# Another order of TensorE's products within a pair of tiles

## What is computed

```python
W = weights[condition]
y = jnp.einsum('bct,bcd->bdt', x, W)
z = jnp.einsum('bsd,od->bso', y, W0) + b
u = jnp.einsum('bsd,edr->ebsr', y, A)
m = jnp.einsum('ebsr,ero,e->bso', u, B, p_scores)
norm_z = jnp.linalg.norm(z, axis=-1, keepdims=True)
norm_m = jnp.linalg.norm(m, axis=-1, keepdims=True)
gamma = jnp.minimum(0.5 * norm_z / (norm_m + 1e-6), 1.0)
out = x + z + gamma * m
```

## Time and profile before

| what | value |
|---|---|
| median of 3 runs | 920.68 us (920.51 to 920.72) |
| the profiled execution | 920.52 us, its span 918.5 us |
| mean granted TensorE clock | 0.999 |
| matmuls, busy | 908.7 us, 99% |
| weight loads, busy | 772.6 us, 84% |
| VectorE, ScalarE, POOL, busy | 587.4, 366.8, 320.6 us |

### The profile page before, as it was taken

One profiled execution on the slowest core, in us unless ns is written; L12 is line 12 of the kernel. 1 busy time (PEld: TensorE's weight loads), 2 busy tenths in 40 slices (PEclk: granted clock), 3 DMA queues, 4 the chain that ended last, 5 costly groups with the idle time before them and its releaser, 6 DMA issues.

```text
span 918.5 us, 14733 instructions
## 1 busy us (share of the span) xinstructions
PE 908.7 (99%) x4628; PEld 772.6 (84%) x4628; DVE 587.4 (64%) x930; ACT 366.8 (40%) x727; POOL 320.6 (35%) x317
## 2 busy tenths in 40 slices
PE   8999999999999999999999999999999999999997
PEld 6888888888888888888888888888888888888885
DVE  6995766566665557665566656666655766566665
ACT  6653443434334334434343343334333433433342
POOL 0123443224433234432344332444323443224432
PEclk9999999999999999999999999999999999999999
DMA  8212222122221222211222212222112222022211
GB/s 304 71 71 94 93 74 77 40 94 94 71 94 47 71 94 79 86 67 50 94 94 71 93 43 74 94 71 94 54 63 94 94 71 88 36 88 94 73 47 69
DMA packets 32744, 75.16 MB, mean 82 GB/s; under 512 B 12761, under 2 KB 13786, under 8 KB 32730
## 3 DMA queue, kind: packets, MB, share of 16 engines
q1 hardware_dynamic: 32138, 73.91, 22.7%
q10 hardware_dynamic: 592, 1.08, 0.3%
HBM read 41.42 MB, written 33.55 MB: 82 GB/s over the span
## 4 chain that ended last, share of the span: by engine, by line
PE 97%; DMA 1%; SPq 0%; DVE 0%; ACT 0%; POOL 0%; issue 0%; DVEq 0%; POOLq 0%
PE b_ps L903 37%; PE c_ps L903 19%; PE mix_ps L890 12%; PE a_ps L903 10%; PE m_ps L962 9%; PE u_ps L943 6%; PE u_ps L947 3%; PE m_ps L903 1%; DMA w_hi_raw<-in_L_ffn_W_dram 1%; POOL stats L372 0%; DMA cond_ids<-in_itok_B_dram 0%; SPq L270 0%; SPq L244 0%; ACT squares L583 0%; DVE z L882 0%
## 5 line engine op out<-in xcount | busy, mean ns | idle before, releaser
L431 ACT CAST y<-mix_ps 128x512 fp32r<-128x512 f32 x126 | 74.4, 591 | 297.9 <-PE mix_ps L890 297.9
L367 POOL TENSOR_TENSOR stats<-stats 128x1 f32<-128x1 f32 x32 | 17.7, 553 | 451.0 <-ACT squares L484 451.0
L903 PE MATMUL b_ps<-w_hi,y 128*128 128x512 f32 x512 | 168.5, 390 | 0.6 <-DVE w_lo L606 0.6
L672 DVE TENSOR_TENSOR s_lo<-s,s_hi 128x512 fp32r<-128x512 f32 x124 | 134.3, 1102 | 4.1
L890 PEld LDWEIGHTS mix_ps<-mixer,x_in 128*128 128x128 f32 x1008 | 122.0, 191 | 6.4 <-issue 1.7
L890 PE MATMUL mix_ps<-mixer,x_in 128*128 128x128 f32 x1008 | 122.7, 275 | 0.5 <-DMA mixer<-in_L_cond_weights_dram 0.5
L444 ACT CAST s_hi<-s 128x512 fp32r<-128x512 f32 x124 | 76.7, 618 | 114.7 <-POOL s L341 93.2
L353 POOL TENSOR_TENSOR z<-z,x_in 128x512 f32<-128x512 f32 x61 | 79.0, 1295 | 113.5 <-ACT squares L465 107.1
L903 PEld LDWEIGHTS b_ps<-w_hi,y 128*128 128x128 f32 x512 | 96.1, 188 | 21.2 <-ACT w_hi L415 1.0
L651 DVE TENSOR_TENSOR y<-mix_ps,y 128x512 fp32r<-128x512 f32 x126 | 86.5, 687 | 39.8 <-ACT s L437 39.6
L903 PE MATMUL b_ps<-w_lo,y 128*128 128x512 f32 x256 | 99.6, 389 | 0.0
(11 more groups left out here) (118 smaller groups left out, 1566.8 us busy)
## 6 DMA issues: line engine op xcount, KB each, us to landing
x_in<-in_x_dram SPq DMA_DIRECT2D x63, 512.0 KB, 3.5
out_dram<-z SPq DMA_DIRECT2D x62, 512.0 KB, 2.8
w_lo_raw<-in_L_ffn_W_dram SPq DMA_DIRECT2D x8, 256.0 KB, 6.2
mixer<-in_L_cond_weights_dram SPq DMA_DIRECT2D x126, 16.0 KB, 2.1
w_hi_raw<-in_L_ffn_W_dram SPq DMA_DIRECT2D x7, 256.0 KB, 6.2
out_dram<-z SPq DMA_DIRECT2D x3, 256.0 KB, 2.0
x_in<-in_x_dram ACTq DMA_DIRECT2D x1, 512.0 KB, 3.2
a_lo_raw<-in_L_ffn_A_dram SPq DMA_DIRECT2D x1, 512.0 KB, 8.1
```

The lines of the kernel that those rows point to most:

```text
L431: nc.scalar.copy(y_part(y_hi, r, h), source(h)).then_inc(y_hi_ready, 1)
L672: nc.vector.tensor_tensor(s_lo[:, n, :, :], s_raw(n), s_hi[:, n, :, :].bitcast(fp32), ALU.subtract).then_inc(s_lo_ready, 1)
L903: summed = nc.tensor.matmul(bank, left[:, k, :], right[:, n, k, :], start=(start and k == 0 and i == 0), stop=(stop and k == HC - 1 and i ...
```

## The change

TensorE's order in a pair becomes P1, P4, P2, up 0, down, mix 0, P6, P5, P7, mix 1, up 1, P3. The down product does its eight wide passes first and its eight narrow ones last, in the prologue too, where a wait on the low part of y falls away since that was waited for earlier. ScalarE squares m before it copies u. VectorE adds P4's bias ahead of `make_z11`, makes the sum of u behind `add_m0`, and makes u2 behind the two y splits of the next tile 0. For the pair p = 1 the sum of u and u2 are taken out of the prologue and made by `step` in the same places as for any other pair.

```diff
--- before.py
+++ after.py
@@ -563,8 +563,8 @@
                     square_z11(p, j, False)
                     if first:
                         split_s(p, S4, True)
+                    square_m0(p - 1, first)
                     copy_u(p, False)
-                    square_m0(p - 1, first)
                     split_u(p)
                     if not closing:
                         for h in range(2):
@@ -811,10 +811,8 @@
             nc.vector.tensor_tensor(s14[:, 1, :, :], s14[:, 1, :, :], s23[:, 0, :, :], ALU.subtract).then_inc(s4_made, 1)
             split_t(T3, 0)
             dve.wait_ge(bias_difference_ready, 1)
-            sum_u(1)
             add_p4_bias(1)
             split_t(T3, 1)
-            make_u2(1, 1)
             split_s(1, S4)
 
             def step(i, first, last):
@@ -832,17 +830,16 @@
                         bias_p1(p, j)
                         for n in (S3, S1, S4):
                             split_s(p, n)
+                        add_p4_bias(p)
                         make_z11(p, j)
-                        sum_u(p)
-                        add_p4_bias(p)
                     make_gamma(p - 1, 0)
                     add_m0(p - 1, 1 - j)
+                    sum_u(p)
                     split_u(p)
-                    if not first:
-                        make_u2(p, j)
                     if not closing:
                         for h in range(2):
                             split_y(p + 1, 0, h)
+                    make_u2(p, j)
                     make_u3(p, j)
                     dve.wait_ge(p4_biased, p)
                     dve.wait_ge(u3_ready, p)
@@ -934,22 +931,15 @@
                 pe.wait_ge(u_hi_ready, p + 1)
                 pe.wait_ge(u_lo_ready, p + 1)
 
-            def down(p):
-
-
-
-                def both(k):
-
-                    return nc.tensor.matmul(u_ps[:, :], a_hi[:, k, :], y[:, k, :, :], start=(k == 0), stop=(k == KC - 1))
-
-                both(0)
+            def down():
+
+
+
                 for k in range(KC):
-                    nc.tensor.matmul(u_ps[:, 0:2 * P], a_lo[:, k, :], y[:, k, 0, :], start=False, stop=False)
-                for k in range(1, HC):
-                    both(k)
-                pe.wait_ge(y_lo_ready, halves(2 * p + 1, 1))
-                for k in range(HC, KC):
-                    summed = both(k)
+                    summed = nc.tensor.matmul(u_ps[:, :], a_hi[:, k, :], y[:, k, :, :], start=(k == 0), stop=(k == KC - 1))
+                for k in range(KC):
+                    summed = nc.tensor.matmul(u_ps[:, 0:2 * P], a_lo[:, k, :], y[:, k, 0, :], start=False,
+                                              stop=(k == KC - 1), skip_group_check=True)
                 summed.then_inc(u_done, 1)
 
             def up(r, m):
@@ -1000,8 +990,7 @@
                 plain(bank, r, 1, W21)
             pe.wait_ge(a_hi_ready, 1)
             pe.wait_ge(a_lo_ready, 1)
-            pe.wait_ge(y_lo_ready, halves(1, 0))
-            down(0)
+            down()
             plain(c_ps[:, :], 0, 1, W22)
             pe.wait_ge(x_loaded[2], 16)
             pe.wait_ge(mixer_loaded[0], 32 * PER)
@@ -1030,16 +1019,7 @@
                         pe.wait_ge(u3_ready, p - 1)
                     product_y(b_ps, 0, 0, W11).then_inc(p_done[1], 1)
 
-                    pe.wait_ge(y_hi_ready, halves(2 * p + 1, 1))
-                    pe.wait_ge(y_lo_ready, halves(2 * p + 1, 0))
-                    down(p)
-
-                    pe.wait_ge(p1_biased, p)
-                    product_y(b_ps, 0, 1, W21, False).then_inc(p_done[2], 1)
-
-                    pe.wait_ge(out1_ready, p)
-                    up(0, m_ps)
-
+                    y_ready(2 * p + 1, 1)
                     if first:
                         pe.wait_ge(z21_ready, 1)
                         pe.wait_ge(t_hi_ready, t_count(T4, 1))
@@ -1048,15 +1028,23 @@
                         pe.wait_ge(p4_biased, p - 1)
                     product_y(a_ps, 1, 1, T4).then_inc(p_done[4], 1)
 
+                    pe.wait_ge(p1_biased, p)
+                    product_y(b_ps, 0, 1, W21, False).then_inc(p_done[2], 1)
+
+                    pe.wait_ge(out1_ready, p)
+                    up(0, m_ps)
+
+                    down()
+
+                    if not closing:
+                        mix_next_0(i, j, p)
+
                     s_ready(p, S2)
                     if first:
                         pe.wait_ge(t_hi_ready, t_count(T2, 1))
                         pe.wait_ge(t_lo_ready, t_count(T2, 1))
                     pe.wait_ge(z11_ready, p + 1)
                     product_s(b_ps, S2, T2).then_inc(p_done[6], 1)
-
-                    if not closing:
-                        mix_next_0(i, j, p)
 
                     s_ready(p, S1)
                     if first:
```

## The result

The changed kernel takes **928.35 us** (median of 4 runs, 927.61 to 928.78) against 920.70 for the kernel before (920.51 to 921.99): ratio 1.0081, 95% interval 1.0069 to 1.0093. It is slower by 7.6 us where 4.0 were forecast, and lies above the stated range of 922.2 to 927.8. The profiled execution took 928.69 us, its span is 926.9 us, 8.4 more than before.

The account below looks back on a forecast made before the run. The prediction took TensorE to bound every pair, with VectorE nearly as full only in the first. It summed 920.52 + 4.9 - 0.7 = 924.7 us, with a range of 922.2 to 927.8.

Parts of the forecast that it names:

- first rival: TensorE's clock falls to 1.2 GHz in the gap before the first pair's P7, slowing its passes: 927.4 us, chance 0.32.
- The row speaks for neither side: At the kernel's end the clock fell 4.9 us after the last matmul; the gap before P7 is also 4.9 us.
- the clock case: Clock falls in the gap before the first pair's P7: 925.5 to 927.4 us, chance 0.32; its full price entered the range.
- +2.7 us: Extra time if all 12 passes of the first pair's P7 run at the lower clock, 0.22 us more per pass.
- +4.9 us, once: First pair: TensorE stands still before P7, waiting for the late u2 on VectorE; bounds 4.7 and 5.2 us.
- norm m on POOL ends at 59.42: First pair: POOL's norm is done early enough for gamma at 59.19 as needed and add m0 at 59.90.
- -0.7 us: Pairs 2 to 30: one narrow-to-wide return less after the down product, 0.024 us a pair; net bounds +1.9 and -3.3.
- Who becomes late in a middle pair: Middle pairs: no operand comes late under the new order; u2 has 1.5 us of slack before P7, costing nothing.
- Nothing gives it back: After the first pair's stall, later pairs have no TensorE idle time to absorb the 4.9 us.

Follow-up runs that it names:

- run 4: Kernel before, TensorE's order kept; only in the first pair VectorE makes the sum of u behind add m0 and u2 behind the y splits: 927.99 us.
- run 2: Changed kernel, but in the first pair VectorE makes u2 right behind the low part of u, ahead of the two y splits: 925.39 us.
- run 3: Changed kernel, but in the first pair u2 is back in its old place on VectorE; the sum of u stays behind add m0: 922.16 us.
- run 1: Changed kernel with 20 extra matmuls of 512 columns, results thrown away, on TensorE just ahead of P7 in the first pair: 926.76 us.
- run 8: Changed kernel with the first pair's lists as before and the down product's narrow passes back in second place: 919.93 us once, 921.71 us when timed again.
- run 10: Kernel before, old TensorE order, but the down product's narrow passes come last, so that P2 follows them: 920.3 us (one run).
- run 6: TensorE's list of the changed kernel with every other engine's list of the kernel before: 921.83 us, ratio 1.0010.
- run 7: Changed kernel with the first pair's lists as before, and SP waiting for P6's end before storing tile 0: 920.39 us (one run).

## Why the prediction was wrong

Its mechanism, one stall of P7 behind a late u2 in the first pair, was right. What was wrong is the choice between the forecast and its first rival, and two sizes. The clock alone would have left the time inside the range (927.4 by the prediction's own rival); that it came out above 927.8 took the two sizes as well, for the range added only 0.4 us to the clock case.

- *"The row speaks for neither side"*, and then the forecast took that the clock holds. **This is the step that failed**, worth 2.4 us in P7 and 0.1 in the mix behind it, of the 3.65 us by which the time was missed. The one row used was the end of the kernel, where the clock fell 4.9 us after the last matmul, and the gap was worked out as just that long. In the changed kernel it fell 4.0 us after the last matmul (60.64 to 64.7), in run 4 after 3.3 (60.29 to 63.6), and in run 2 it fell 4.3 after the last matmul before the gap though work had come back for 1.3 us by then. A single row of a fall is a sample and not a limit, and it was too little for 0.53 on the side on which the clock holds. The rule of the Trainium skill that the prediction set against the row (TensorE: Matmul & The Clock Gate, "Why this matters for your kernels") was the better guide. The traces agree with it: the clock was lost in the 5.3 us gap and even behind the 3.0 us one, and it held over 1.1 us (run 3).
- *"+2.7 us"*, the rival's price, was measured by P7's 5.26 - 2.83 (60.36 to 63.19 before) = 2.4 us. Right within its bound; a pass at the lower clock takes 0.43, not 0.45.
- *"+4.9 us, once"*, with bounds of 4.7 and 5.2: P7 came 5.61 us later than before. Of the miss, the first part is *"norm m on POOL ends at 59.42"*. It ended at 57.56 + 2.13 = 59.69, so gamma waited 0.44 us and add m0 started at 60.44 and not 59.90: 0.54. The instruction is a single column that takes 0.55 us in a middle pair; here VectorE ran L642 and L672 beside it, each reading two operands from SBUF, without a pause until 59.29. Before, and in run 3, u2 stood between the two, which reads one of its operands from PSUM, and POOL ended 0.41 us behind L642; in the changed kernel and in runs 1, 2 and 4 it ended 0.40 to 0.41 us behind L672. So the prediction, which let POOL's instruction start 0.3 us earlier and end no later, did not see that taking u2 out of that place would itself hold up the norm. The Trainium skill (GPSIMD Engine Reference, "1. Specifications") has POOL's SBUF interfaces shared with VectorE, with contention when a VectorE instruction has two SBUF inputs. The traces agree with it in the two ends above. The chain from add m0 to u2 was worked out as 5.32 us and took 5.38 (60.44 to 65.82), and the start of P7 came 0.15 behind it in place of 0.06.
- *"-0.7 us"* for 29 pairs without a return to wide passes. The down product did take 2.77 in place of 2.79. The mix behind the narrow passes took its 1.70, as before. But P6 took 0.03 more than the product behind a mix did before (2.85 against 2.82), so a pair came out at +0.007 us, +0.2 in all. The term was worked out for the border next to the down product alone, and the price came one product later; both bounds held.
- *"Who becomes late in a middle pair"*: nobody, as said. In the pair from 415.18 on, VectorE took up P4's bias at 422.84 right behind the splits, and u2 was done at 433.10, 1.6 us ahead of P7 at 434.74, where 1.5 was worked out.
- *"Nothing gives it back"*: so it was.

The parts then add up to what was seen: forecast 4.2 (4.9 - 0.7), clock 2.5, longer stall 0.7, middle pairs 0.9 (from -0.7 to +0.2) make 8.3. The profiled executions differ by 8.2 us and their spans by 8.4; the medians differ by 7.65.

## What to carry to other kernels

A change to a list that is right for every repetition of a loop is to be checked on the first repetition by itself, since there an engine may still be full of other work: here 7 us came from two instructions that lost their place ahead of a long chain, in one pair of 32. Here stalls of TensorE of 3.0, 5.3 and 5.4 us were followed by the lower clock and stalls of 0.7 and 1.1 us were not; nothing in between was run. A stall of 3 us or more is to be priced with the lower clock behind it, nearly half as much again here (2.5 on 5.6 us), and a stall that was shortened to 3 us is to be priced so too. Where passes of different width are reordered, the saving at one border has to be looked for at the next one.

## What the runs showed of the hardware that I had not expected

- The clock fell while matmuls were running again, 1.3 us after the end of a 3.0 us gap (run 2), and stayed low for 3.4 us. In the changed kernel and in run 4 it stayed low for 6.8 us. Over gaps of 0.7 and 1.1 us (runs 1 and 3) it held.
- With 24 short passes in one run ahead of a product (8 of 256 columns, 16 of 128), its last 11 passes took 2.53 us, 0.03 more than with 16 alone (P5 behind a mix in the kernel before: 452.19 to 454.69, 2.50; P6 of run 8: 308.12 to 310.62, 2.50). With 8 alone they took 2.51 (P2 of run 10, 412.47 to 414.98). It is neither the store nor the work of other engines beside them (runs 6 to 8). What holds the wide passes up is left open.
- A POOL instruction on one column took 2.13 us, four times its 0.55 in a middle pair, beside two VectorE instructions back to back that each read two operands from SBUF, and ended 0.40 us behind the second. With an instruction between them that reads one operand from PSUM it took 1.53 to 1.59 us and ended 0.41 us behind the first. One such instruction in between, moved elsewhere, makes POOL late.
